# Choosing PSUM banks by when a score's bank counts as given back

## The chip, the cores and the metric

One core of one Trainium2 chip runs the whole program. The metric is the device time of one execution in microseconds (us), as the median of several runs. The engines are TensorE (PE, and PEld for its weight loads), VectorE (DVE), ScalarE (ACT), GpSimd (POOL) and SyncE (SP), which here only issues transfers. TensorE writes its products to PSUM, which has eight banks of 128 x 512 float32; VectorE and ScalarE read them there.

## The reference

Four attention layers follow one another on an image batch of 8 samples, 256 channels and 32 x 32 = 1024 places, all in float32. Cut to what matters:

```python
def layer_0_or_2(x):                      # layer 2 adds to xn in place of x
    xn = group_norm(x) * w + b
    q, k, v = split(qkv_w @ xn + qkv_b)   # 8 heads of 32 channels
    a = softmax(q.T @ k / sqrt(32)) @ v   # for each head, 1024 x 1024 scores
    return x + proj_w @ a + proj_b

def layer_1(x):
    y = group_norm(x) + pos_emb
    s = y * sigmoid(conv1(silu(conv3(silu(conv1(y))))))
    n = group_norm(y)
    standard = attention(n, n, n)         # 8 heads of 32
    multi = [attention(s, n, n) for _ in range(2)]        # 2 heads of 128
    f = out_w @ (ff_w2 @ silu(ff_w1 @ concat(standard, multi) + ff_b1) + ff_b2) + out_b
    return group_norm(f) + x

def layer_3(x):                           # one head of 256 channels
    q, k, v = split(qkv_w @ group_norm(x) + qkv_b)
    return x + out_w @ (softmax(q.T @ k / 16) @ v) + out_b
```

## The kernel before, in words

For each sample there are five attentions, called kinds: 0 (layer 0), 1 and m (the standard and the multi part of layer 1), 2 (layer 2) and 3 (layer 3). Kinds 0, 1 and 2 are narrow (four heads of 32 channels side by side), m and 3 are wide (heads of 128 or 256 channels). An attention goes in steps over 512 queries, a step in units. A unit is one product of 128 keys by 512 queries, the *score*: 32 units a step and 4 steps in a narrow attention, 8 units a step in a wide one. There are 3,456 scores in all.

What belongs to a unit on the engines: TensorE makes the score in a bank, ScalarE reads it and writes its exponential to `probs` (L852), GpSimd adds the exponentials up (L1166, L1179), and some units later TensorE makes the value products into a bank named `av` and, once a step, the sums into a bank named `sums`. At the end of a step VectorE turns the sums (L984), takes their reciprocal (L988), turns back (L992) and multiplies `av` with it (L1007). In a narrow attention that is at units 34 to 37 of the next step.

So that the exponential can't overflow, each step needs the maximum of its scores first. It is taken from approximate products made ahead, for the step that comes next: in a narrow attention TensorE makes them in *quads* (`quad`), four products of 32 x 128 at once from `high_parts`, one in each of four banks, and VectorE reduces each of the four (L962, `max_cols`), one a unit. In a wide attention they are made one by one (`maximum`). A small transpose (`columns`, L659) brings the maxima to where the scores need them.

Between these stand the pieces of the other work of the samples, with due times in units written by hand (`stages`): group norms, projections for q, k and v (which ScalarE reads twice, L927 and L928), output projections (`proj`, read at L1098), the feed-forward part and the convolutions. Two samples are in work at a time: while one is in an attention, the other does the work between. `plan` merges all of it into one list, `PLAN`, which every engine runs through in order. Each engine is a queue of its own in that order and waits on semaphores.

PSUM: each bank has a semaphore `full`, raised by the last matmul into it, and a semaphore `read`, raised by its reader. TensorE gets a bank with `take` (L522). It never asks whether the bank is free: the choice is made when the program is built, from counts of turns (`count["turn"]`, one up at every `take` and every `give`), and the program then waits until the last user's read is done. A bank taken with `hold` (`av`, `sums`, quads, projections) can't be chosen until `give` is reached in the plan, which is where the plan has its read. Scores, wide maxima and columns are taken without `hold`, and count as given back in the turn of their `take`. The choice is the bank with the smallest `given`.

Of the kernel before, what the change touches and what calls it, by code (L numbers as in the profile page):

```python
# [28 lines left out]
TAIL = 13  # L29
BANKS = 8  # L30
ADDED = 6

RESIDENT = [("sa1", 192), ("sa2", 96), ("sa3", 128), ("ident", P), ("gmean", P)]
for _n in ("0", "pre", "norm", "post", "2", "3"):
# [26 lines left out]
class Attention:  # L61


    def __init__(self, kind, turn, sample):
# [5 lines left out]
        self.units = self.steps * self.per  # L70
        self.adds = 7 if self.wide else 2 * (ADDED - 1)
        self.maxima = QT * NH * (1 if self.wide else GROUP)
# [278 lines left out]
def added_before(att, item):  # L351
# [3 lines left out]
    s, i = divmod(item, 8)  # L355
    return att.adds0 + att.adds * s + 2 * max(1, i) if i < ADDED else 0

# [12 lines left out]
def build_program(nc, x, pos, resident, stream, fold, out):  # L370
    ctx = ExitStack()
    with ctx:
# [113 lines left out]
        def until_full(eng, key):  # L486
            bank, _, n = tiles[key]
            eng.wait_ge(full[bank], n + 1)
            return PS[bank]
# [25 lines left out]
        def _(pe):  # L515
# [2 lines left out]

            count = {"ws": 0, "h": 0, "gn": 0, "turn": 0}
            uses, fulls, given, held = [0] * BANKS, [0] * BANKS, [0] * BANKS, {}  # L520

            def take(key, hold=False, says_full=True):  # L522

                bank = min((i for i in range(BANKS) if i not in held.values()), key=lambda i: (given[i], i))
                tiles[key] = bank, uses[bank], fulls[bank]
                if uses[bank]:
                    pe.wait_ge(read[bank], uses[bank])
                uses[bank] += 1
                fulls[bank] += says_full
                count["turn"] += 1  # L530
                given[bank] = count["turn"]
                if hold:
                    held[key] = bank
                return PS[bank]
# [8 lines left out]
            def score(att, u):  # L543
                s, r = divmod(u, att.per)
                if r == 0:
                    pe.wait_ge(row_ready, 16 * (att.step0 + s + 1))
                    if not att.wide:
                        pe.wait_ge(stacked[s], stacks_done(att, s))
                    if u == 0 and att.wide:
                        pe.wait_ge(lo_ready, 8 * (att.index + 1))  # L550
                key = ("score", att.index, u)
                bank = take(key)
                if att.wide:
                    qs, ks = half(s % NH), slice(r * P, (r + 1) * P)
                    for ct in range(att.ctiles):
                        g = att.head(s) + ct
                        k_hi, k_lo = (wide_part(att.kind, "k", part)[:, g, ks] for part in ("hi", "lo"))
                        q_hi, q_lo = (wide_part(att.kind, "q", part)[:, g, qs] for part in ("hi", "lo"))
                        mm(bank[:, :], k_hi, q_hi, ct == 0, False)
                        mm(bank[:, :], k_hi, q_lo, False, False)  # L560
                        mm(bank[:, :], k_lo, q_hi, False, False)
                    mm(bank[:, :], ONEROW[:, :], NR[:, s % 2, :], False, True).then_inc(filling(key), 1)
                else:
                    kt, j = divmod(r, GROUP)
                    mm(bank[:, :], KS[0:97, GROUP * att.head(s) + j, kt * P:(kt + 1) * P],
                       QS[0:97, att.buf(s), j, :], True, True).then_inc(filling(key), 1)

            def sums(bank, probs, start, stop):
                for j in range(GROUP):
                    ins = mm(bank[D * j:D * j + D, :], ONES[:, 0:D], probs[:, j, :], start, stop,  # L570
                             tile_position=(0, D * j))
                return ins

            def narrow_probs(att, s, i):
                return PR[:, (att.item0 + 8 * s + i) % P_RING, :, :]

            def values_narrow(att, s, i):
                until_read(pe, ("score", att.index, 32 * s + 4 * i + 3))
                key = ("av", att.index, s)
                if i == 0:  # L580
                    take(key, True)
                bank, probs = PS[tiles[key][0]], narrow_probs(att, s, i)
                for j in range(GROUP):
                    h = GROUP * att.head(s) + j
                    ins = mm(bank[D * j:D * j + D, :], VT[:, att.index % 2, i, D * h:D * h + D], probs[:, j, :],
                             i == 0, i == 7, tile_position=(0, D * j))
                if i < ADDED:
                    ins.then_inc(p_used, 1)
                if i == 7:
                    ins.then_inc(filling(key), 1)  # L590

            def sums_narrow(att, s, part):
                key = ("sums", att.index, s)
                if part < 2:
                    if part == 0:
                        take(key, True)
                    sums(PS[tiles[key][0]], narrow_probs(att, s, ADDED + part), part == 0, False).then_inc(p_used, 1)
                else:
                    pe.wait_ge(p_added, att.adds0 + att.adds * (s + 1))
                    sums(PS[tiles[key][0]], ADD, False, True).then_inc(filling(key), 1)  # L600
# [124 lines left out]
            for i, (first, second) in enumerate((("ff2", "ffo"), ("wv3", "wp3"))):  # L725
                bank = take(("fold", i))
# [5 lines left out]
            bank = take(("fold", 2))  # L732
# [8 lines left out]
            for event, it, i in PLAN:  # L741
# [4 lines left out]
                elif event == "mean":  # L746
                    key = ("mean", it.sample, i)
                    bank = take(key, True)
# [3 lines left out]
                elif event == "var":  # L752
                    key = ("var", it.sample, i)
                    bank = take(key, True)
# [380 lines left out]
        def _(pool):  # L1135
# [17 lines left out]
            def score(att, u):  # L1153
# [13 lines left out]
                else:  # L1167
                    i, j = divmod(r, 4)
                    if not 1 <= i < ADDED or j % 2 == 0:
                        return  # L1170
# [62 lines left out]
        def _(sp):  # L1233
# [4 lines left out]
            for _, between in SLOTS:  # L1238
                if between is not None:
                    order += {"1": ["p0", "1"], "3": ["p2", "3"], "2": ["ff", "2"]}.get(between.kind, [between.kind])  # L1240
# [195 lines left out]
```

## Time and profile before

| | us |
|---|---|
| median of 3 runs | 5362.62 (5360.14 to 5363.67) |
| the profiled execution | 5362.61 |
| its span, first to last instruction | 5360.8 |
| TensorE busy | 4897.9 (91%) |
| VectorE, ScalarE, GpSimd busy | 2833.4, 2577.3, 3268.5 |
| mean granted clock of TensorE | 0.948 of full |

A row of the timeline has the start in us from the span's start, the duration, the engine, the line, the operation, what is written from what, and in brackets how long the engine was idle before it and which instruction ended that. Neighbouring instructions of one kind are merged (x4), and the duration is then of all. A row of waits tells for whom an engine waited, how long in total, how often, and the longest.

### The profile page before, as it was taken

To read this page: it belongs to the slowest core of one execution; us is meant where nothing else is said; L and a number is where in the kernel's file an instruction comes from. 1 tells how busy PE (TensorE), PEld (TensorE's weight loads), DVE (VectorE), ACT (ScalarE), POOL (GpSimd) and SP (SyncE) were. 2 spreads that over 40 slices of the span, in tenths; PEclk is the share of its full clock that TensorE was granted. 3 is DMA by queue.
4 is the path that set the end of the run, shared out by engine and by line. 5 is a ranking of instruction groups with operands and counts; after the bars stand their busy time and mean duration, and the time that the engine had idled before them with its cause. 6 is when DMAs were issued, how large, how long until landed. Compare 5 with 4: busy or idle time off the path is not lost. (4 is left out here: it accounts for less than half of the span.)

```text
span 5360.8 us, 63346 instructions
## 1 busy us (share of the span) xinstructions
PE 4897.9 (91%) x22016; PEld 2258.4 (42%) x22016; DVE 2833.4 (53%) x5112; ACT 2577.3 (48%) x4641; POOL 3268.5 (61%) x1969
## 2 busy tenths in 40 slices
PE   7788899998999989999899989999899998999887
PEld 3235333543335433354334543345334453345434
DVE  5354566255662566535664366644566345662362
ACT  3353565435563456624555246552556525554252
POOL 4473677546674567735777357763677636776363
PEclk8799999999899999999999999999999999999898
DMA  3111211021210221102210122201122012120010
GB/s 86 29 31 51 52 46 41 20 54 45 50 35 20 60 54 39 36 22 66 51 46 20 35 53 56 48 13 45 43 56 54 7 50 56 42 50 11 19 45 12
DMA packets 103608, 221.20 MB, mean 41 GB/s; under 512 B 31104, under 2 KB 33408, under 8 KB 103168
## 3 DMA queue, kind: packets, MB, share of 16 engines
q1 hardware_dynamic: 103296, 217.16, 15.7%
q8 instruction: 181, 2.97, 0.2%
q14 instruction: 131, 1.07, 0.1%
HBM read 56.47 MB, written 8.39 MB: 12 GB/s over the span
## 5 line engine op out<-in xcount | busy, mean ns | idle before, releaser
L962 DVE TENSOR_REDUCE max_cols<-bank 128x1 f32<-128x512 f32 x3456 | 2182.5, 680 | 1742.1 <-PE bank L517 1736.9
L852 ACT ACTIVATE probs<-bank 128x512 f32<-128x512 f32 x3456 | 1931.5, 600 | 2332.9 <-PE bank L517 2130.4
L1179 POOL TENSOR_TENSOR probs_added<-probs_added,probs 128x1024 f32<-128x1024 f32 x768 | 1799.8, 2374 | 61.9 <-ACT probs L852 61.7
L517 PE MATMUL bank<-q_stack,k_stack 97*128 97x512 f32 (+1 forms) x3584 | 1655.1, 518 | 82.9 <-DVE max_cols L962 35.5
L517 PE MATMUL bank<-probs,v_tokens 128*32 128x512 f32 (+1 forms) x7168 | 1374.3, 634 | 49.9 <-ACT probs L852 49.9
L517 PEld LDWEIGHTS bank<-q_stack,k_stack 97*128 97x128 f32 (+1 forms) x3584 | 657.9, 194 | 768.8 <-issue 383.6
L517 PE MATMUL bank<-act,weight_stream 128*128 128x512 f32 x1792 | 926.0, 617 | 24.4 <-ACT probs L852 6.9
L1179 POOL TENSOR_TENSOR probs_added<-probs 128x1024 f32<-128x1024 f32 x192 | 453.7, 2368 | 681.0 <-ACT probs L852 670.8
L1166 POOL TENSOR_TENSOR probs_added<-probs 128x512 f32<-128x512 f32 x48 | 61.1, 1273 | 757.6 <-PE bank L517 725.2
L517 PEld LDWEIGHTS bank<-probs,v_tokens 128*32 128x32 f32 (+1 forms) x7168 | 322.4, 122 | 475.2 <-issue 315.2
L517 PE MATMUL bank<-high_parts 32*128 32x512 f32 x3072 | 402.6, 512 | 130.9 <-DVE max_cols L962 96.5
L517 PEld LDWEIGHTS bank<-high_parts 32*128 32x128 f32 x3072 | 157.6, 188 | 761.4 <-issue 706.2
L517 PEld LDWEIGHTS bank<-act,weight_stream 128*128 128x128 f32 x1792 | 326.2, 193 | 319.9 <-issue 282.4
L1166 POOL TENSOR_TENSOR probs_added<-probs_added,probs 128x512 f32<-128x512 f32 x288 | 373.4, 1297 | 119.3 <-ACT probs L852 95.2
L1230 POOL TENSOR_TENSOR low_parts<-full_parts,high_parts 128x512 fp32r<-128x512 f32 x192 | 244.7, 1280 | 110.3 <-ACT full_parts L928 110.3
L517 PE MATMUL bank<-k_stack 128*128 128x512 f32 x512 | 269.2, 564 | 28.0 <-ACT probs L852 21.6
L517 PE MATMUL bank<-weight_stream,act 128*128 128x256 f32 x1024 | 263.2, 386 | 7.3 <-DVE max_cols L962 7.3
L984 DVE STREAM_TRANSPOSE sums_turned<-bank 128x512 f32<-128x512 f32 x144 | 101.7, 706 | 309.9 <-PE bank L517 309.9
L517 PEld LDWEIGHTS bank<-weight_stream,act 128*128 128x128 f32 x1024 | 186.8, 189 | 87.9 <-issue 53.6
L974 DVE CAST neg_max_t<-bank 16x128 fp32r<-16x128 f32 (+1 forms) x144 | 39.6, 275 | 325.0 <-PE bank L659 324.9
L517 PE MATMUL bank<-q_stack 128*128 128x512 f32 x512 | 204.7, 456 | 3.6 <-DMA neg_row<-neg_max_t 2.1
L862 ACT ACTIVATE act<-act,gn_shift,gn_scale 128x512 f32<-128x512 f32 x192 | 151.0, 814 | 100.5 <-POOL gn_shift L1197 100.5
(85 smaller groups left out, 3336.1 us busy)
## 6 DMA issues: line engine op xcount, KB each, us to landing
k_stack<-high_parts SPq DMA_DIRECT2D x384, 128.0 KB, 2.4
q_stack<-high_parts SPq DMA_DIRECT2D x768, 64.0 KB, 2.0
weight_stream<-stream_dram SPq DMA_DIRECT2D x32, 768.0 KB, 4.3
k_stack<-low_parts SPq DMA_DIRECT2D x192, 128.0 KB, 2.4
q_stack<-low_parts SPq DMA_DIRECT2D x384, 64.0 KB, 2.0
act<-x_dram SPq DMA_DIRECT2D x8, 1024.0 KB, 6.5
act<-pos_dram SPq DMA_DIRECT2D x8, 1024.0 KB, 5.8
weight_stream<-stream_dram SPq DMA_DIRECT2D x16, 512.0 KB, 3.7
```

Of the source, the lines that this page charges most:

```text
L517: return nc.tensor.matmul(dst, lhsT, rhs, start=start, stop=stop, **kw)
L852: act.activation(PR[:, m % P_RING, j, :], bank[:, :], ACT.Exp, scale=att.scale).then_inc(reading(key), 1)
L862: act.activation(act_buf(it.turn, dst)[:, t, half(nh)], act_buf(it.turn, src)[:, t, half(nh)], ACT.Identity, scale=GA[:, t:t + 1], bias=GS ...
L962: dve.tensor_reduce(cols[:, kh, j, qt:qt + 1], bank[:, :], AX.X, ALU.max).then_inc(reading(key), 1)
L974: dve.tensor_copy(NT_[0:att.cols, :], bank[0:att.cols, 0:P]).then_inc(reading(key), 1)
L984: dve.transpose(RT[:, :], bank[:, :]).then_inc(reading(key), 1)
L1166: pool.tensor_tensor(ADD[:, 0, :], one, two, ALU.add).then_inc(p_added, 1)
L1179: pool.tensor_tensor(ADD[:, js, :], one, two, ALU.add).then_inc(p_added, 1)
L1230: pool.tensor_tensor(low, whole, high.bitcast(F32), ALU.subtract).then_inc(lo_ready, 1)
```

## The change

A new list `scored` remembers whether a bank's last user was a score. `take` adds `SCORE_LATE` = 3 turns to `given` of such a bank when it compares. Nothing else is changed: the order of all instructions, their operands apart from the bank, and the kinds of waits stay.

```diff
+SCORE_LATE = 3
...
             uses, fulls, given, held = [0] * BANKS, [0] * BANKS, [0] * BANKS, {}
+            scored = [False] * BANKS
 
             def take(key, hold=False, says_full=True):
 
-                bank = min((i for i in range(BANKS) if i not in held.values()), key=lambda i: (given[i], i))
+
+                bank = min((i for i in range(BANKS) if i not in held.values()),
+                           key=lambda i: (given[i] + SCORE_LATE * scored[i], i))
+                scored[bank] = key[0] == "score"
                 tiles[key] = bank, uses[bank], fulls[bank]
                 if uses[bank]:
                     pe.wait_ge(read[bank], uses[bank])
```

## Rows read from the trace of the kernel before

**Rows 1.** The page: engines' busy time, then the granted clock in 40 slices.

```profile
PE 4897.9 (91%) x22016; PEld 2258.4 (42%) x22016; DVE 2833.4 (53%) x5112; ACT 2577.3 (48%) x4641; POOL 3268.5 (61%) x1969
...
PEclk8799999999899999999999999999999999999898
```

**Rows 2.** TensorE's waits, whole span (released by: us in total, times, longest).

```profile
PE bank L517 <- DVE max_cols L962: 149.1, 203, 4.4
PE bank L517 <- ACT probs L852: 123.7, 162, 3.6
PE bank L517 <- DVE mean_var L1071: 48.9, 19, 8.9
PE bank L517 <- DVE dev_squared L1084: 17.3, 12, 2.0
```

**Rows 3.** The page's costliest groups: narrow scores and quads (busy, mean ns, idle before).

```profile
L517 PE MATMUL bank<-q_stack,k_stack 97*128 97x512 f32 (+1 forms) x3584 | 1655.1, 518 | 82.9 <-DVE max_cols L962 35.5
...
L517 PE MATMUL bank<-high_parts 32*128 32x512 f32 x3072 | 402.6, 512 | 130.9 <-DVE max_cols L962 96.5
```

**Rows 4.** TensorE's waits from 2478 to 3126 us, one sample's period.

```profile
PE bank L517 <- DVE max_cols L962: 17.9, 26, 4.3
PE bank L517 <- ACT probs L852: 12.2, 19, 3.6
```

**Rows 5.** The timeline, kind 2 (start, duration, engine, idle before in brackets).

```profile
2670.26 1.27 DVE L962 TENSOR_REDUCE max_cols<-bank 128x1 f32<-128x512 f32 x2
...
2671.07 0.50 PE L517 MATMUL bank<-high_parts 32*128 32x512 f32 x4 [0.39 <-DVE max_cols L962]
```

**Rows 6.** The timeline at units 38 and 39, kind 2.

```profile
2686.49 0.51 PE L517 MATMUL bank<-high_parts 32*128 32x512 f32 x4 [0.28 <-ACT probs L852]
2686.94 0.65 DVE L962 TENSOR_REDUCE max_cols<-bank 128x1 f32<-128x512 f32 x1
2687.51 0.67 DVE L1007 TENSOR_TENSOR act<-bank,sums_turned 128x512 f32<-128x512 f32 x1
...
2687.64 1.69 PE L517 MATMUL bank<-q_stack,k_stack 97*128 97x512 f32 x4 [0.65 <-DVE max_cols L962]
```

**Rows 7.** The timeline at units 58 and 59, kind 0.

```profile
2553.12 0.50 PE L517 MATMUL bank<-q_stack,k_stack 97*128 97x512 f32 x1
...
2554.44 0.67 DVE L962 TENSOR_REDUCE max_cols<-bank 128x1 f32<-128x512 f32 x1
...
2557.98 0.67 DVE L962 TENSOR_REDUCE max_cols<-bank 128x1 f32<-128x512 f32 x1
...
2558.91 0.80 PE L517 MATMUL bank<-high_parts 32*128 32x512 f32 x4 [4.29 <-DVE max_cols L962]
2559.20 0.67 DVE L962 TENSOR_REDUCE max_cols<-bank 128x1 f32<-128x512 f32 x1
```

**Rows 8.** The timeline at a quad behind a query projection, kind 1.

```profile
2882.84 0.69 ACT L928 ACTIVATE full_parts<-bank,weights 128x512 f32<-128x512 f32 x1
...
2882.90 0.51 PE L517 MATMUL bank<-high_parts 32*128 32x512 f32 x4
```

**Rows 9.** The timeline at a wide maximum, kind m.

```profile
3043.05 0.81 ACT L862 ACTIVATE act<-act,gn_shift,gn_scale 128x512 f32<-128x512 f32 x1 [8.18 <-POOL gn_shift L1197]
3043.78 0.58 ACT L852 ACTIVATE probs<-bank 128x512 f32<-128x512 f32 x1
...
3044.40 0.80 PE L517 MATMUL bank<-k_stack 128*128 128x512 f32 x1 [3.61 <-ACT probs L852]
```

**Rows 10.** Stretches: us, then busy us (count) of PE, PEld, DVE, ACT, POOL, then PEclk, DMA share, GB/s.

```profile
2534.00:2544.00 10.00, 9.83 (x34) 4.11 (x34) 6.11 (x15) 4.26 (x8) 7.00 (x4) 0.52 0.01 2
...
2686.00:2696.00 10.00, 8.63 (x47) 3.23 (x43) 9.96 (x21) 5.74 (x11) 9.58 (x6) 1.00 0.05 13
...
3043.00:3049.00 6.00, 4.60 (x7) 2.17 (x8) 0.69 (x1) 4.37 (x7) 3.77 (x4) 0.50 0.36 145
```

## Prediction

> **What bounds the kernel now.** I read the page first: TensorE is busy 91% of the span and no other engine over 61%, so the order of work on TensorE and its pauses make the time; its granted clock is full speed in most slices, and in several nine tenths or less [rows 1]. Then who TensorE waits for: reads of maxima by VectorE (149.1 us) and of scores by ScalarE (123.7 us) lead the list; the statistics chains behind them (48.9 and 17.3 us) are no matter of banks [rows 2]. The groups show where: the group that holds the narrow scores idles 82.9 us and the quads (four maxima products, one bank each, from `high_parts`) 130.9 us [rows 3]. So pauses on banks are a few per cent of the span, and whatever the new rule does is done there. The work repeats for each sample, so I laid out one period, 2478 to 3126 us. In it TensorE waits 17.9 us for maxima and 12.2 us for scores [rows 4].
>
> **What the rule changes.** No instruction is added or removed. `take` (L522) gives the bank that was given back longest ago. A score's bank counts as given back when the score is *made*, a narrow maximum's at the planned place of its *read* (`give`), though the read itself may be late. Now a score's bank counts three turns younger. I went through the plan with both rules on paper: there are 8,115 takes and 4,128 gives, so a turn lasts 5360.8 / 12,243 = 0.44 us on average and three are 1.3 us. Of the takes, 7,087 get another bank and 5,608 follow another predecessor: the change does what it says. What grows younger is what stands before a quad: 204 of the 768 narrow quads contain the bank of the very last maximum of the quad before; with the new rule it is 549. Each wait stands in TensorE's queue in order, so everything behind it waits too, and ScalarE and VectorE are fed late. SyncE's transfers and GpSimd's sums only follow.
>
> The price of each new predecessor is read off the period thus: the end of the read of the new predecessor, less the time at which TensorE could have begun without its wait of today.
>
> *Quads that wait for one more maximum.* VectorE ends two maxima in a row at 2670.26 + 1.27 = 2671.53, and the quad starts at 2671.07 after 0.39 us of waiting for the first of them, which ends 0.6 us before the second [rows 5]. Under the new rule its fourth bank is that of the second. It can start some 0.5 us later. The same stands at the second quad before this one, at the one before that without a wait today, and three times in the next attention: 6 x 0.53 = 3.2 us.
>
> *The score after the normalisation.* At units 38 and 39 of a step VectorE is behind, as transposes, reciprocal and normalisation stand among its maxima. Score 39 starts at 2687.64 after 0.65 us, behind a maximum that ends at 2687.59; the new rule gives it the bank of `av`, which VectorE reads until 2687.51 + 0.67 = 2688.18 [rows 6]. That is 0.6 us later. The quad before it would also wait, for 1.2 us more, but as both wait for the same run of VectorE only the later end counts. Four such places at 0.6, three milder at 0.3 to 0.5: 3.5 us.
>
> *The quad behind GpSimd.* In kind 0, VectorE stops for statistics whose data GpSimd makes, and a quad waits 4.29 us, to 2558.91, for the maximum that ends at 2557.98 + 0.67 = 2558.65. The new predecessor is the next one, ending at 2559.20 + 0.67 = 2559.87, 1.2 us later; as today's start already stands some 0.2 us behind the read, I count 1.05 us. The score at 2553.12 follows a score now and would follow the maximum ending at 2554.44 + 0.67 = 2555.11, 2.0 us later, but that goes into the wait behind it [rows 7]. Together 1.05 us.
>
> *Quads that follow a projection.* At 2882.90 a quad starts without a pause; its new fourth bank is read by ScalarE's second pass over a query product, from 2882.84 for 0.69 us, so it starts 0.68 us late [rows 8]. There are three such quads (0.5, 0.7, 0.7) and nine other takes of 0.1 to 0.6 us with other predecessors: 5.3 us.
>
> *Scores and columns that now follow a maximum:* a dozen places of 0.15 to 0.6 us, 3.0 us in all; several come in a row and wait for a VectorE that does not depend on the pause before. Half counts: 1.5 us.
>
> *What goes away.* The longest wait for a score is 3.61 us, for a wide maximum at 3044.40. ScalarE stands behind the group norm until 3043.05 and reads the score at 3043.78 [rows 9]. The new bank is long free. But the next unit's value product needs that same score, so only the work between, a maximum, a value product, a projection part and a score, comes ahead of the wait: some 2.0 us. Six or seven smaller waits for scores go too: 2.5 us. Together -4.5 us.
>
> *Sum for a sample:* 3.2 + 3.5 + 1.05 + 5.3 + 1.5 - 4.5 = +10.0 us. With the starting and closing samples incomplete I count 7.5 of them: +75 us.
>
> **Bounds.** Upward: if every lateness counts in full and none goes into another's, the period gives +23 us, the kernel about +175 us. Downward: if all new lateness is swallowed by later waits and the removed ones count in full (3.6 + 2.5 us), -6 x 7.5 = -45 us. I take +75, as the examples in [rows 5, 6, 8] are separate places with TensorE busy in between, and keep both ends for the range.
>
> **The clock.** The stretch behind score 39 of the first step of kind 0 ran at half clock (0.52, the 1.2 of the two levels 1.2 and 2.4 GHz), where pauses of 0.35, 0.6 and 1.1 us lay close together; the same place of kind 2, with smaller pauses, kept the full clock (1.00); behind the 3.61 us wait it was 0.50 [rows 10]. So new pauses can cost a half-clock stretch of some 10 us, about 5 us of work, and a removed one can save some 3 us. Two candidate places a sample, each at one in two, against one removed: +2 us a sample, which I leave out of the sum and keep for the range.
> The Trainium skill (TensorE: Matmul & The Clock Gate, A second HAM failure mode: psum-queue depth-cycling) says that small idle times between matmul groups, from cycling through PSUM banks, can make the clock swing and cost more than their own length. By that rule the result would be rival A below; the trace agrees at two of the three places just named.
> The Trainium skill (Perfetto Trace Analysis, Matmuls) wants independent groups to rotate through the banks so that the reading of one overlaps the next. By it alone both rules would be alike, as both use all eight banks; that is rival C. The trace speaks against it: at the places above the take comes less than 0.6 us behind the read that it needs, and one step in the rotation moves that read by about as much.
>
> **Rivals.**
> A. *The clock tips.* As forecast, and two to three more half-clock stretches a sample at 4 to 5 us: +75 + 2.5 x 4.5 x 7.5 = +160, about 5523 us. For it [rows 10]; against it, that many half-clock stretches follow pauses over 1 us and most new ones are 0.5 us.
> B. *Faster: scores are the late ones.* ScalarE reads in order and can stand long behind another wait (8 us at 3043), while VectorE's new shortfalls are half a microsecond and lie before waits that swallow them. Then the removed waits decide: -6.1 us a sample, -3 for a half-clock stretch saved, +3 left of the new ones: -6 x 7.5 = -45, about 5318 us. It decides as soon as less than 4.5 of the 14.5 us of new lateness survives. For it, 12.2 us of waits for scores in the period [rows 4]; against it, the long one returns at the value product, and only about half of the others get an earlier predecessor.
> C. *No difference.* Waits change name from ScalarE to VectorE. It needs new lateness to survive to a third.
>
> **How the numbers follow.** The profiled execution took 5362.61 us, 1.8 us over its span, and the median of three is 5362.62: no correction. Forecast 5362.6 + 75 = 5438 us. Chances: the forecast's mechanism between about +11 and +130 us 0.62; A 0.12; B 0.15; C 0.11. Faster by over 0.2% (10.7 us, about what a measurement can tell from no change) 0.15, within 0.11, slower 0.74. The range leaves out the upper half of A and most of B: 5345 to 5525.
>
> **What would show it.** In the profile after: waits for maxima in a period rise from 17.9 to over 25 us and waits for scores fall from 12.2 to 8 or 9; new waits for `av` (L1007) and for ScalarE's L928 of some 0.6 us appear; `high_parts` idles clearly over 130.9 us; the longest wait for a score stays 1.5 to 2 us long, one unit later. Busy times and counts stay. If the sum of TensorE's waits for VectorE doesn't grow by 50 us, the forecast's mechanism is wrong; if it does and the time stays, the lateness was swallowed; if the mean clock falls under 0.94, A holds.

## The result and the profile after

| | before | after |
|---|---|---|
| median of 5 runs | 5362.62 us | 5437.94 us |
| lowest and highest | 5351.33, 5368.75 | 5430.32, 5472.34 |
| the profiled execution | 5362.61 | 5472.34 |

The ratio is 1.0154, with a 95% interval of 1.0132 to 1.0176: the change makes the kernel 1.5% slower. 5438 us was forecast. The profiled execution is the slowest of the five, so what its rows add up to (110 us over the span before) is more than the 75 us of the medians.

The page of the changed kernel (its first line, the engines, the granted clock in 40 slices), to be held against [rows 1]:

```profile
span 5470.6 us, 63346 instructions
...
PE 4950.5 (90%) x22016; PEld 2273.1 (42%) x22016; DVE 2839.7 (52%) x5112; ACT 2575.3 (47%) x4641; POOL 3271.9 (60%) x1969
...
PEclk8899989998999999999889999999989999899988
```

TensorE is busy 4950.5 us in place of 4897.9 with the same 22,016 matmuls, and idle 5470.6 - 4950.5 = 520.1 us in place of 5360.8 - 4897.9 = 462.9. So of the 110 us in this execution 57 are pauses and 53 are the same matmuls done more slowly; the mean granted clock is 0.938 in place of 0.948.

TensorE's waits over the whole span (total us, times, longest), against [rows 2]:

```profile
PE bank L519 <- DVE max_cols L968: 205.7, 269, 2.8
PE bank L519 <- ACT probs L858: 47.9, 70, 3.1
PE bank L519 <- DVE mean_var L1077: 42.4, 19, 8.9
PE bank L519 <- ACT act L868: 39.4, 9, 6.4
PE bank L519 <- ACT full_parts L934: 25.6, 40, 1.8
...
PE bank L519 <- DVE act L1013: 17.2, 21, 1.1
PE bank L519 <- DVE group_mean L1093: 15.7, 7, 2.2
```

The lines of the readers are six further down than before, and TensorE's L517 is now L519: L968 is the maximum's read (L962 before), L858 the exponential (L852), L1013 the read of `av` (L1007), L934 ScalarE's second read of a projection (L928), L868 the group norm's scaling (L862). Waits for scores fell by 76 us, from 123.7 to 47.9. Waits for maxima rose by 57, and behind them stand causes that hardly existed: the projections' second read (25.6; 5.7 before), the group norm's scaling (39.4; 11.2 before), `av` (17.2; 1.2 before), `group_mean` (15.7) and `sums_turned` (7.2), which were not there.

The groups of [rows 3] (busy, mean ns, idle before), and the one of the projections:

```profile
L519 PE MATMUL bank<-q_stack,k_stack 97*128 97x512 f32 (+1 forms) x3584 | 1683.3, 527 | 53.4 <-DVE max_cols L968 29.7
...
L519 PE MATMUL bank<-act,weight_stream 128*128 128x512 f32 x1792 | 931.1, 620 | 46.7 <-ACT act L868 34.5
...
L519 PE MATMUL bank<-high_parts 32*128 32x512 f32 x3072 | 410.1, 520 | 213.0 <-DVE max_cols L968 153.2
```

Scores wait less (53.4 us; 82.9 before), quads much more (213.0; 130.9 before). That is the change in one sentence: it takes pauses from the scores and gives more of them to the quads. Beside it the products of wide maxima lost 21 us of pauses and the projections got 22 (24.4 to 46.7 us): that is the long wait of rows 9, which only moved (see wide_only).

Where in a sample the time goes is seen from stretches that each hold one attention, from its first score to the next one's (the columns are those of rows 10). Before, kinds 0, 2, 1 and m:

```profile
2477.80:2644.00 166.20, 150.10 (x714) 61.43 (x712) 98.49 (x181) 92.84 (x168) 117.70 (x68) 0.94 0.21 52
2644.00:2797.90 153.90, 144.43 (x729) 56.10 (x730) 103.98 (x189) 92.06 (x169) 115.80 (x67) 0.97 0.20 49
2797.90:2934.20 136.30, 129.14 (x671) 53.93 (x672) 75.85 (x136) 81.82 (x150) 101.23 (x54) 0.96 0.13 34
...
3013.20:3126.20 113.00, 102.88 (x349) 59.08 (x348) 56.15 (x105) 33.06 (x56) 41.48 (x37) 0.95 0.16 43
```

After, kind 2 of the sample before, and then the same four:

```profile
2023.50:2185.70 162.20, 148.33 (x729) 56.94 (x730) 104.22 (x189) 91.83 (x169) 117.64 (x69) 0.94 0.19 46
...
2513.30:2681.70 168.40, 153.09 (x714) 61.84 (x712) 98.77 (x180) 92.94 (x168) 117.39 (x68) 0.92 0.20 51
2681.70:2854.60 172.90, 158.98 (x729) 59.70 (x729) 104.34 (x188) 91.91 (x169) 117.67 (x69) 0.87 0.18 43
2854.60:2988.90 134.30, 124.27 (x671) 52.84 (x672) 76.00 (x136) 81.86 (x150) 100.10 (x53) 1.00 0.14 34
...
3067.90:3182.20 114.30, 102.10 (x349) 58.73 (x348) 56.29 (x105) 33.09 (x56) 41.51 (x37) 0.97 0.16 42
```

Length less PE busy is the idle time. It changes by -0.8 us in kind 0 (16.1 to 15.3), +4.5 in kind 2 (9.5 to 13.9), +2.9 in kind 1 (7.2 to 10.0) and +2.1 in m (10.1 to 12.2): +8.6 us a sample. Kind 3 takes 79.0 us without a pause in both. Busy time changes by +3.0, +14.6, -4.9 and -0.8: +11.9 us in the sample shown, and by the same sums only +1.2 in the sample before it. In kind 1 the clock is whole (1.00; 0.96 before) and that pays more than its pauses cost. In kind 2 it falls from 0.97 to 0.87, or to 0.94 in the sample before. These two stretches of kind 2 have the same instructions and, within 0.1 us, the same idle time (13.9 us); they differ by 10.7 us in length, all of it in the clock.

### The profile page after: what moved, and what is told of

It is laid out like the page before. It is cut to its first block and busy times, and to the rows that moved or that the text cites. A ratio compares the mean times of both kernels' runs of the same rounds, so it can differ in the third digit from the quotient of the medians.

```text
span 5470.6 us, 63346 instructions
## 1 busy us (share of the span) xinstructions
PE 4950.5 (90%) x22016; PEld 2273.1 (42%) x22016; DVE 2839.7 (52%) x5112; ACT 2575.3 (47%) x4641; POOL 3271.9 (60%) x1969
## 5 line engine op out<-in xcount | busy, mean ns | idle before, releaser
L968 DVE TENSOR_REDUCE max_cols<-bank 128x1 f32<-128x512 f32 x3456 | 2185.5, 681 | 1855.8 <-PE bank L519 1852.0
L858 ACT ACTIVATE probs<-bank 128x512 f32<-128x512 f32 x3456 | 1929.5, 600 | 2444.4 <-PE bank L519 2290.7
L519 PE MATMUL bank<-q_stack,k_stack 97*128 97x512 f32 (+1 forms) x3584 | 1683.3, 527 | 53.4 <-DVE max_cols L968 29.7
L519 PE MATMUL bank<-probs,v_tokens 128*32 128x512 f32 (+1 forms) x7168 | 1390.8, 644 | 60.2 <-ACT probs L858 44.3
L519 PEld LDWEIGHTS bank<-q_stack,k_stack 97*128 97x128 f32 (+1 forms) x3584 | 670.7, 198 | 740.7 <-issue 409.8
L519 PE MATMUL bank<-act,weight_stream 128*128 128x512 f32 x1792 | 931.1, 620 | 46.7 <-ACT act L868 34.5
L519 PE MATMUL bank<-high_parts 32*128 32x512 f32 x3072 | 410.1, 520 | 213.0 <-DVE max_cols L968 153.2
L519 PEld LDWEIGHTS bank<-probs,v_tokens 128*32 128x32 f32 (+1 forms) x7168 | 322.2, 122 | 501.1 <-issue 328.0
L519 PEld LDWEIGHTS bank<-high_parts 32*128 32x128 f32 x3072 | 161.4, 191 | 868.3 <-issue 820.8
L519 PEld LDWEIGHTS bank<-act,weight_stream 128*128 128x128 f32 x1792 | 326.4, 194 | 341.8 <-issue 313.7
L519 PE MATMUL bank<-k_stack 128*128 128x512 f32 x512 | 268.5, 565 | 6.7 <-DMA neg_row<-neg_max_t 6.7
L519 PE MATMUL bank<-weight_stream,act 128*128 128x256 f32 x1024 | 263.2, 386 | 7.3 <-DVE max_cols L968 7.3
L519 PEld LDWEIGHTS bank<-weight_stream,act 128*128 128x128 f32 x1024 | 186.8, 189 | 87.8 <-issue 53.8
L519 PE MATMUL bank<-q_stack 128*128 128x512 f32 x512 | 204.8, 456 | 3.6 <-DMA neg_row<-neg_max_t 2.1
L868 ACT ACTIVATE act<-act,gn_shift,gn_scale 128x512 f32<-128x512 f32 x192 | 150.9, 813 | 98.7 <-POOL gn_shift L1203 98.7
```

The source lines that it names most:

```text
L519: return nc.tensor.matmul(dst, lhsT, rhs, start=start, stop=stop, **kw)
L858: act.activation(PR[:, m % P_RING, j, :], bank[:, :], ACT.Exp, scale=att.scale).then_inc(reading(key), 1)
L868: act.activation(act_buf(it.turn, dst)[:, t, half(nh)], act_buf(it.turn, src)[:, t, half(nh)], ACT.Identity, scale=GA[:, t:t + 1], bias=GS ...
L968: dve.tensor_reduce(cols[:, kh, j, qt:qt + 1], bank[:, :], AX.X, ALU.max).then_inc(reading(key), 1)
```

## Experiments

All times are medians on the chip, each beside runs of the kernel before on the same chip. "Idle" is span less PE busy of the profiled execution and "busy" is PE busy, both as differences from before (462.9 and 4897.9). The profiled execution is seldom the median one, so these two need not add up to the change in the median. Diffs are against the changed kernel, but for half_before, order and order2, which are against the kernel before.

| kernel | change in us (ratio, 95% interval) | idle | busy |
|---|---|---|---|
| late1 | +14 (1.0031, 1.0018 to 1.0045) | 0 | +14 |
| late2 | +64 (1.0125, 1.0099 to 1.0150) | +25 | +35 |
| three turns (the change) | +75 (1.0154, 1.0132 to 1.0176) | +57 | +53 |
| late5 | +267 (1.0503, 1.0482 to 1.0524) | +112 | +157 |
| kind2 | +70 (1.0141, 1.0115 to 1.0168) | +27 | +34 |
| quads_only | +87 (1.0158, 1.0140 to 1.0176) | +48 | +30 |
| no_quads | +15 (1.0028, 1.0015 to 1.0042) | -5 | +25 |
| quads_of_2 | +60 (1.0114, 1.0085 to 1.0143) | +17 | +46 |
| wide_only | -1 (1.0000, 0.9989 to 1.0011) | +6 | -5 |
| half_before | -46 (0.9916, 0.9897 to 0.9935) | -17 | -29 |
| half_after | -14 (0.9976, 0.9964 to 0.9988) | +27 | -43 |
| order | -26 (0.9949, 0.9932 to 0.9965) | -50 | +27 |
| order2 | -62 (0.9886, 0.9869 to 0.9903) | -54 | -7 |

**How many turns.** My theory was that the time follows how often a take lands on a bank whose read is not over. The rival was that the old order just fitted, and that any reshuffling costs. The same line has 2 in late2 and 5 in late5.

```diff
-SCORE_LATE = 3
+SCORE_LATE = 1
```

> SCORE_LATE = 1 in place of 3. My theory is that the time follows how often a take lands on a bank whose read is not over yet: with one turn only 316 quads hold the bank of the last maximum of the quad before (204 before the change, 549 with three turns), and as many waits for scores go as waits for maxima come. It expects 0 to +20 us on the kernel before. The rival that any reshuffling of the banks costs, because the old order happened to fit, expects about the +75 us of three turns. The rival that the clock alone is the cause has no number of its own; it expects the mean granted clock to go with the time.

> SCORE_LATE = 2. By my theory the cost grows with the count of such quads (460 of 768, between 316 and 549): +30 to +55 us on the kernel before. Any-reshuffle rival: +75 us. A rival that has a threshold between two and three turns expects less than 15 us.

> SCORE_LATE = 5. By my theory the cost goes on growing, as more takes land on maxima, av and sums that are not read: +110 to +180 us on the kernel before, with waits for VectorE well over 250 us in the trace. The rival that the quads' fourth bank is all there is expects little more than three turns give, since 549 of 768 are hit already: +75 to +95 us.

One turn costs 14 us, two 64, three 75, five 267. That any reshuffling costs doesn't fit the first: counted in the plan, one turn gives 6,916 takes another bank, three 7,087. But only 2,216 takes follow another predecessor with one turn and 5,608 with three, so it is order, further down, that settles this rival. That the clock alone is the cause doesn't fit either: the mean granted clock does go with the time (0.946, 0.940, 0.938 and 0.923 in the profiled executions), but so do the pauses, and order is faster than the kernel before at 0.945. Two turns are above what I gave them and five far above: quads with the bank of the last maximum before them only go from 549 to 663 of 768, and the cost more than triples. So the time doesn't go in proportion to this count. TensorE's waits with five turns:

```profile
PE bank L519 <- DVE max_cols L968: 184.6, 327, 2.0
PE bank L519 <- DVE act L1013: 69.2, 48, 2.5
...
PE bank L519 <- DVE neg_max_t L980: 24.4, 14, 3.5
```

The maxima alone have 184.6 us, less than with three turns. But `av`, read at the very end of a step, now has 69.2, and the columns' read, `neg_max_t`, 24.4: the rule reaches for banks that were given back last of all. And it is not the pauses that grow most:

```profile
span 5630.1 us, 63346 instructions
...
PE 5054.7 (90%) x22016; PEld 2302.1 (41%) x22016; DVE 2839.6 (50%) x5112; ACT 2580.8 (46%) x4641; POOL 3271.4 (58%) x1969
```

The same matmuls take 157 us more than before, against 112 us of pauses. The Trainium skill (TensorE: Matmul & The Clock Gate, A second HAM failure mode: psum-queue depth-cycling) says that small pauses between groups of matmuls, as a kernel cycles through its banks, make the clock swing and cost beyond their own length. The trace agrees here: 157 us beside 112, at a mean granted clock of 0.923 in place of 0.948.

**Which kind.** The trace of the changed kernel has the added time in kind 2.

```diff
-                scored[bank] = key[0] == "score"
+                scored[bank] = key[0] == "score" and ATTS[key[1]].kind == "2"
```

> Three turns, but only for banks last used by a score of kind 2; the scores of the other kinds count as before the change. In the trace of the changed kernel the stretch of kind 2 is 8 to 19 us longer a sample, kind 0 is 2 us longer, m 1 us longer and kind 1 is 2 us shorter. If the cost belongs to the places in kind 2, this kernel shows it nearly whole: +60 to +80 us. If it is spread as my count of late reads had it (a third of it in each narrow kind), it shows +20 to +35 us.

+70 us: with the scores of one narrow kind in three, nearly the whole. My count of late reads, by which each narrow kind bears about a third, is wrong in this.

**Which takes.**

```diff
+                quad_take = key[0] == "max" and not ATTS[key[1]].wide
                 bank = min((i for i in range(BANKS) if i not in held.values()),
-                           key=lambda i: (given[i] + SCORE_LATE * scored[i], i))
+                           key=lambda i: (given[i] + SCORE_LATE * (scored[i] and quad_take), i))
```

For `no_quads` it is `not quad_take`, for `quads_of_2` `quad_take = key[0] == "max" and ATTS[key[1]].kind == "2"`.

> The three turns are added only where a narrow quad takes its banks; all other takes choose as before the change. If the quads' fourth bank is the main cost, this shows most of the +75 us: +40 to +80. The rival that the other takes (scores landing on maxima and on av) carry it expects under +20 us here.

> The three turns are added for every take but those of narrow quads. Theory of the quads: +0 to +25 us on the kernel before. The rival that scores which land on av and on maxima carry the cost: +40 us or more.

> The three turns are added only where a quad of kind 2 takes its banks (256 of the 768 narrow quads). In the traces of the three turns for all, of the kernel with kind 2's scores alone and of the one with the quads alone, the added time stands in the stretch of kind 2. If it is made by kind 2's own quads, this kernel is 45 to 80 us slower than the kernel before. If quads of the other kinds or other takes share in it, it is under 30 us.

The quads alone cost +87 us, everything else alone +15, and the quads of kind 2 alone +60. The two parts don't add up to the whole (+75); each choice changes the turns that the next one compares, but no run takes this apart. The cost is the quads', and most of it that of kind 2's. In the profiled execution of quads_of_2 only a quarter of it is pauses: of a span of 5424.5 us TensorE is busy 4944.2, 46 over before, and idle 480.3, 17 over.

**What VectorE's reads have to do with it.** If quads wait because VectorE reads the last maximum of the quad before only just then, shorter reads must take the cost away.

```diff
-                dve.tensor_reduce(cols[:, kh, j, qt:qt + 1], bank[:, :], AX.X, ALU.max).then_inc(reading(key), 1)
+                n = HALF // 2 if att.kind == "2" else HALF
+                dve.tensor_reduce(cols[:, kh, j, qt:qt + 1], bank[:, 0:n], AX.X, ALU.max).then_inc(reading(key), 1)
```

> The kernel before, but VectorE takes the maximum of a kind 2 row over 256 of its 512 scores (half of each of kind 2's maxima is left out; the others are whole). It is the base for half_after. Fewer waits for maxima in kind 2, of which there are some 4.5 us in a period: 0 to 25 us faster than the kernel before.

> The changed kernel (three turns) with the same shortened maxima of kind 2 as half_before (half of each of kind 2's maxima is left out). Theory: the quads of kind 2 wait because VectorE reads the last maximum of the quad before only just then; with reads some 0.25 us shorter each, four in a row end about 1 us earlier and most of the waits of 0.5 to 1 us go. It expects half_after less half_before at most +30 us, against +75 for the whole maxima. The rival that the new order costs through something else than the length of VectorE's reads (ScalarE's reads, projections, the clock for itself) expects +60 to +80 again.

Both kernels leave out half of each of kind 2's maxima. half_after less half_before is 5349.0 - 5317.6 = +31 us, just over the 30 that I gave at most, against +75 with whole maxima: the length of reads in kind 2 makes more than half of the cost. But the way is another than I wrote. The pages of half_before and of half_after:

```profile
span 5314.2 us, 63346 instructions
...
PE 4868.8 (92%) x22016; PEld 2255.8 (42%) x22016; DVE 2565.6 (48%) x5112; ACT 2573.4 (48%) x4641; POOL 3268.9 (62%) x1969
```

```profile
span 5345.3 us, 63346 instructions
...
PE 4855.4 (91%) x22016; PEld 2259.0 (42%) x22016; DVE 2569.3 (48%) x5112; ACT 2571.4 (48%) x4641; POOL 3269.4 (61%) x1969
```

Idle time still rises by 489.9 - 445.4 = 44 us, where it rose by 57 with the whole maxima. What is gone is the slowing of the matmuls: busy falls by 13 us where it rose by 53. (That 53 is of the slowest execution; for the median one some 18 is my estimate, worked out below. The matmuls then make 31 of the 44 us that the shorter reads save, the pauses 13.) The stretch of kind 2, in half_before and then in half_after:

```profile
2629.50:2781.30 151.80, 144.79 (x729) 56.29 (x729) 80.74 (x189) 91.83 (x169) 117.30 (x69) 0.96 0.20 49
```

```profile
2646.30:2799.60 153.30, 143.77 (x729) 56.73 (x730) 80.74 (x188) 91.74 (x169) 118.51 (x70) 0.96 0.20 49
```

Kind 2 has 7.0 us of idle time in the one and 9.5 in the other, so the added pauses there are 2.5 us in place of 4.5, and the granted clock holds at 0.96. half_before itself gained 46 us where I gave it at most 25, 29 of them in the matmuls.

**The long wait in kind m.**

```diff
-SCORE_LATE = 3
+SCORE_LATE = 1
...
-                scored[bank] = key[0] == "score"
+                scored[bank] = key[0] == "score" and ATTS[key[1]].wide
```

> Only banks last used by a score of a wide attention count late, by one turn. By the read times of the trace before, this takes away the 3.6 us wait of kind m (six times) and adds next to nothing. If the wait really goes: -20 us, and up to -40 us with the half-clock stretch behind it. If it comes back at the value product that needs the same score, as my prediction said: -5 to -15 us. If it moves whole: no difference.

No difference. The wait of rows 9 is gone from its place and stands whole at the next matmul that depends on ScalarE: over the whole span, waits for scores fell by 22 us (123.7 to 101.5) and waits for the group norm's scaling rose by 28 (11.2 to 39.3). The timeline of wide_only, with the last score read and the group norm's scaling on ScalarE, and the projection that needs it:

```profile
2394.52 0.81 ACT L868 ACTIVATE act<-act,gn_shift,gn_scale 128x512 f32<-128x512 f32 x1 [8.19 <-POOL gn_shift L1203]
2395.24 0.58 ACT L858 ACTIVATE probs<-bank 128x512 f32<-128x512 f32 x1
2395.72 2.21 ACT L868 ACTIVATE act<-act,gn_shift,gn_scale 128x512 f32<-128x512 f32 x3
...
2398.03 2.05 PE L519 MATMUL bank<-act,weight_stream 128*128 128x512 f32 x2 [4.67 <-ACT act L868]
```

ScalarE works off one queue: the group norm, the score, then the rest of the group norm until 2397.93. The projection part that stands between the value product and the next score in the plan needs just that. TensorE had been held at the maximum for 3.6 us; now it is held at the projection for 4.67.

**Choosing by the real end of the read.** The last question is whether the distance between read and take is a cause worth working on, or whether waits for banks only change their name. Here `take` chooses by a list of read times, one for each take, from a trace.

```diff
+            read_at, read_by = [int(d) for d in READ_STEPS.split()], [0] * BANKS
+            for n in range(1, len(read_at)):
+                read_at[n] += read_at[n - 1]
...
-                bank = min((i for i in range(BANKS) if i not in held.values()), key=lambda i: (given[i], i))
+                bank = min((i for i in range(BANKS) if i not in held.values()), key=lambda i: (read_by[i], i))
+                read_by[bank] = read_at[sum(uses)]
```

> The kernel before, but take chooses the bank whose last read ended first, by a list of read times (one for each take) from the trace of the kernel before, written into the program in place of the count of turns. If what counts is the distance between the real end of the read and the take, waits for VectorE's maxima and ScalarE's scores fall from 273 us to under 150 us and the time falls by 50 to 130 us. If such a bank wait only hands over to a wait for data behind it, the waits are renamed and the time stays within 15 us. If the time rises, read times of one run don't carry over to a changed order.

> As the kernel order, with the list of read times taken from the trace of order instead of that of the kernel before. If the rest of its bank waits (88 us on scores, 87 on maxima) stands at places where the list no longer fits, it is a further 5 to 30 us faster. If it is as good as such a choice gets with eight banks, it is within 5 us of order, which was 26 us under the kernel before.

The first list, from the trace of the kernel before, gives -26 us, half of the least that I expected; waits for maxima and scores fell from 273 us to 175, not to under 150. It settles the rival of the first experiment: 7,093 takes get another bank and 3,751 another predecessor, and the time falls. It also shows that my count of quads was only a stand-in: 354 of order's quads hold the bank of the last maximum of the quad before, more than the 316 of one turn, which costs 14 us. The second, from the trace of the first, gives -62 us: 5301.28 us, the fastest kernel of this study, faster than both. TensorE's waits in it:

```profile
PE bank L722 <- ACT probs L1061: 95.1, 135, 3.1
PE bank L722 <- DVE max_cols L1171: 86.4, 146, 2.9
PE bank L722 <- DVE mean_var L1280: 59.9, 33, 8.9
```

Waits for scores and maxima are 181.5 us together, 91 under those of rows 2, but the idle time fell by 54 only: the statistics' chain takes 11 back, and waits for which the profile names no releaser rose from 13.4 to 34.9 us. The first list saved almost the same idle time (50 and 54 us), but its matmuls were 27 us slower than before and those of the second 7 us faster. Why the clock held in the one and not in the other, the runs don't show.

## Why the prediction was right, and where it was not

**The size came out, its parts did not.** 5438 us was forecast and 5437.94 measured. The forecast had +10.0 us of pauses a sample and nothing for the clock. The profiled execution has +8.6 us of pauses a sample and, for all samples, 57 us of pauses and 53 of slower matmuls. That the sum was right to a microsecond is luck: two errors met. The pauses came out at 57 us in place of 75, and the clock, which the text priced at +2 us a sample and left out of the sum, cost 53 us in the slowest execution, as much as the pauses. In the others it cost less: they run from 5430 to 5443 us at granted clocks from 0.948 to 0.943. The fastest has the mean clock of the kernel before (0.948) and still takes 68 us more, so the pauses stand there by themselves. If the pauses are 57 us in the median execution too, the clock takes 18 of its 75 us; that is an estimate, as only one execution has a profile, and it is near the 2 x 7.5 = 15 us that were left out. Rival A, which had a chance of 0.12, is what the slowest execution shows in part, though at 110 us and not at 160; it is not what the median shows.

**What bounds the kernel:** right. TensorE's pauses and clock are the whole difference; busy times of the other engines moved by under 7 us.

**Quads that wait for one more maximum:** right in mechanism, a little high in sum. 0.39 us of waiting, plus 0.53, should be 0.92; the quad of [rows 5] now stands here, with the two reads in front of it:

```profile
2708.58 1.27 DVE L968 TENSOR_REDUCE max_cols<-bank 128x1 f32<-128x512 f32 x2
...
2710.00 0.51 PE L519 MATMUL bank<-high_parts 32*128 32x512 f32 x4 [0.99 <-DVE max_cols L968]
```

0.99 us. All six places show 0.7 to 1.0. But at two of them, the quads that had no wait, the score behind had waited 0.75 us for `proj`'s read and now waits 0.22: of their 0.70 us only some 0.17 is new. In sum these places cost 2.7 us where I had 3.2.

**The score after the normalisation:** the mechanism failed in its detail. The wait of [rows 6] was to move to the score behind `av`. It moved to the quad before it, which now waits for the maximum that the score had waited for:

```profile
2732.44 0.51 PE L519 MATMUL bank<-high_parts 32*128 32x512 f32 x4 [0.99 <-DVE max_cols L968]
```

That is 0.99 us, and with 0.21 in front of the value product 1.20, against 0.28 + 0.65 = 0.93 before. So +0.3 where I counted +0.6. I had seen that both wait for the same run of VectorE, but not that after the first wait `av` has been read: the term was twice too high here.

**The quad behind GpSimd:** the wait of [rows 7] was split as described and cost less.

```profile
2590.70 0.79 PE L519 MATMUL bank<-q_stack,k_stack 97*128 97x512 f32 x1 [2.65 <-DVE max_cols L968]
...
2595.66 0.80 PE L519 MATMUL bank<-high_parts 32*128 32x512 f32 x4 [2.30 <-DVE max_cols L968]
```

2.65 + 2.30 = 4.95 us against 4.29 + 0.22 (the latter at the next score): +0.4 where I had 1.05. And the wait for the statistics right behind it took that back. Before and after:

```profile
2563.76 0.56 PE L517 MATMUL bank<-mean_var,weights 128*128 128x2 f32 x2 [2.61 <-DVE mean_var L1071]
...
2599.28 0.56 PE L519 MATMUL bank<-mean_var,weights 128*128 128x2 f32 x2 [1.68 <-DVE mean_var L1077]
```

TensorE comes later and waits 0.9 us less (over the whole span, this wait fell from 48.9 to 42.4 us), so the place gains 0.5 us and the term should have been -0.5. In all, kind 0 has 0.8 us less idle than before.

**Quads that follow a projection:** right. [rows 8] priced the wait for ScalarE's second read at 0.68 us:

```profile
2939.20 0.69 ACT L934 ACTIVATE full_parts<-bank,weights 128x512 f32<-128x512 f32 x1
...
2940.03 0.50 PE L519 MATMUL bank<-high_parts 32*128 32x512 f32 x4 [0.71 <-ACT full_parts L934]
```

0.71 us, and the quad after it the same. Among the other takes of this term, none of which I had over 0.6 us, is one that came to 1.2 (a wait of 1.02 us before, 2.23 now): a quad whose bank is that of a group mean. VectorE does three pieces of the convolution first, then a maximum, then the statistics' small steps (in the plan's order), and the quad waits for the last of them. VectorE's and TensorE's timeline:

```profile
2744.58 2.26 DVE L1117 SCALAR_TENSOR_TENSOR act<-bank,weights,act 32x512 f32<-32x512 f32 x3 [0.30 <-ACT act L890]
...
2746.87 0.69 DVE L968 TENSOR_REDUCE max_cols<-bank 128x1 f32<-128x512 f32 x1
...
2748.05 0.15 DVE L1093 TENSOR_SCALAR group_mean<-bank 128x2 f32<-128x2 f32 x1
...
2748.35 0.50 PE L519 MATMUL bank<-high_parts 32*128 32x512 f32 x4 [2.23 <-DVE group_mean L1093]
```

**What goes away:** the small waits were mis-sized, the long one's step failed. I had the waits for scores in a period falling from 12.2 to 8 or 9 us; they fell to 3.1. For the long wait I looked for the next user of the same *score* and found the value product one unit on. The next work that depended on the same *engine* was nearer, the projection:

```profile
3101.30 1.79 PE L519 MATMUL bank<-act,weight_stream 128*128 128x512 f32 x2 [4.67 <-ACT act L868]
```

4.67 us for the group norm's scaling, where there were 3.61 for the score. So -2.0 should have been 0 or a little above, which wide_only shows alone. Here the forecast failed as a mechanism and not only in size: it followed the score's data and not ScalarE's queue.

**The clock:** this is what the runs add. The forecast gave each of two places a sample one chance in two of an added half-clock stretch. The kernel before has one stretch in kind 2, of 9.7 us, behind waits of 1.02 and 1.65 us:

```profile
2702.00:2711.70 9.70, 8.05 (x20) 2.20 (x19) 4.73 (x9) 2.30 (x4) 8.16 (x6) 0.50 0.00 0
```

The rows for the same two places of kind 2 in the changed kernel, first in the sample where it took 162.2 us and then in that where it took 172.9:

```profile
2054.00:2058.00 4.00, 4.00 (x20) 1.43 (x19) 2.37 (x9) 1.37 (x3) 3.65 (x2) 0.61 0.02 4
2084.40:2098.10 13.70, 11.83 (x30) 3.29 (x30) 6.18 (x11) 2.30 (x4) 8.63 (x9) 0.50 0.00 0
2712.40:2726.10 13.70, 13.70 (x57) 5.13 (x60) 6.38 (x16) 7.04 (x13) 7.28 (x9) 0.50 0.13 31
2750.00:2773.90 23.90, 22.13 (x48) 5.16 (x49) 7.70 (x15) 5.61 (x10) 8.37 (x8) 0.50 0.00 1
```

Both samples have a stretch at half clock (0.50, the 1.2 of the two levels 1.2 and 2.4 GHz) behind the wait of 2.2 us, but one lasts 13.7 us and the other 23.9. And both have one behind the waits of 1.0 us at the two quads before, but in the first it is so short that 4 us around it still show 0.61; in the second it lasts 13.70 us, and TensorE is busy for all of it. The pauses are the same in sum in both. Eight value products take 1.94 us at half clock (at 2591.42) and 1.06 at full (at 2730.39). By that ratio the short stretch, with TensorE busy for 11.83 us, costs about 5 us and the long one, with 22.13, about 10 (estimates), beside pauses of 4 to 4.5 us (2.2 at the quad and about 2 at the next convolution piece). The long one stands in four of the seven samples in this execution's steady part (from 762, 2750, 4080 and 4750 us), so which it is changes from sample to sample. That kind 2 bears the cost is shown by kind2 and quads_of_2. That it is the size and place of its pauses is shown in part, by half_after. Why kind 1, whose first half has the same waits of 0.98 and 0.99 us, got its clock back instead is open.

**What the profile was to show:** waits for maxima in a period, 17.9 before, were to pass 25 us; in the 648 us from 2534 on they are 23.8. `high_parts` passed 130.9 clearly. TensorE's waits for VectorE, summed over all lines of the list, went from 248 to 332 us, over the 50 us that I had named as the test. The mean clock fell just under the 0.94 that I had named for rival A in the slowest execution (0.938), and not in the other four (0.943 to 0.948). The longest wait at a wide maximum did not stay 1.5 to 2 us long: it is 4.67, at the projection. Rival B fell: waits that went came back elsewhere. Rival C fell with the interval.

## What to carry to other kernels

A rule that chooses buffers by planned turns is only as good as its picture of when reads end: making one kind of reader look late pushes the takes onto the others, while taking all readers' times from a trace gained 26 us, and 62 with the list renewed. Before counting a removed wait as gained, look for the next work that depends on the same engine's queue, not only for the next user of the same data. And price a pause on TensorE twice, by its length and by the matmuls at half clock behind it: here the second was about a third of the first in the median execution (an estimate), as large in the slowest, and larger with five turns.

## What was not expected of the hardware

Two samples of one execution with the same instructions and the same pauses (13.9 us) took 162.2 and 172.9 us, with granted clocks of 0.94 and 0.87. Kind 1, with waits of 0.98 and 0.99 us in its first half, kept the whole clock (1.00), and before the change, with waits of 0.39 us at the same quads, it did not (0.96). Five executions of the changed kernel span 42 us, against 17 us for five of the kernel before (24 for sixteen on another chip). With five turns TensorE's matmuls took 157 us longer for 112 us of added pauses.
